# Routed experts on one core: each expert's token shares spread over its partitions by DMA from a scratch in memory, in place of three selection products per block

## The reference, cut to what matters

```
hidden[e] = silu(x @ gate[e]) * (x @ up[e])        # 64 wide
y         = sum over e of  (c[e] * hidden[e]) @ down[e]
```

## Time and profile before

| | before |
|---|---|
| median of 3 runs | 5519.05 us (5516.63 to 5520.13) |
| the profiled execution, its own time | 5518.67 us |
| its span (first to last instruction) | 5516.8 us |
| PE busy, share of the span | 4263.4 us, 77% |
| DVE busy | 3278.4 us, 59% |
| ACT busy | 2686.6 us, 49% |
| POOL busy | 1336.0 us, 24% |
| moved by DMA | 66.82 MB, 12 GB/s on average |
| mean granted TensorE clock | 0.873 |

### The profile page before, as it was taken

The page is one execution under the profiler, slowest core; times in us unless marked ns, Lnnn a source line. Parts: engine busy times, 40 slices in busy tenths (PEclk is TensorE's granted clock), DMA queues, the critical chain, the costliest instruction groups (busy, mean ns, idle before and its releaser), DMA issues. The chain is left out here.

```text
span 5516.8 us, 132549 instructions
## 1 busy us (share of the span) xinstructions
PE 4263.4 (77%) x46246; PEld 2462.1 (45%) x46246; DVE 3278.4 (59%) x5922; ACT 2686.6 (49%) x5526; POOL 1336.0 (24%) x2908
## 2 busy tenths in 40 slices
PE   2013867877669895868996578999999999999997
PEld 0002333433332221443442236666667666666665
DVE  7994434544347675434444426766666676767665
ACT  2125623545447574531111345656656565656564
POOL 0061100111101111110000044434434343434433
PEclk7556977988779897978997678999999999999998
DMA  1000000000000000000110001000000000000000
GB/s 33 0 0 3 2 19 8 1 4 1 17 19 1 1 1 12 2 14 27 30 30 12 5 1 47 6 9 23 6 14 17 5 27 5 10 23 5 27 5 11
DMA packets 46816, 66.82 MB, mean 12 GB/s; under 512 B 8628, under 2 KB 40480, under 8 KB 44977
## 3 DMA queue, kind: packets, MB, share of 16 engines
q1 hardware_dynamic: 45564, 58.16, 3.5%
q0 software_dynamic: 784, 1.80, 0.2%
HBM read 53.22 MB, written 1.05 MB: 10 GB/s over the span
## 5 line engine op out<-in xcount | busy, mean ns | idle before, releaser
L673 DVE TENSOR_REDUCE minus_max<-banks 128x1 f32<-128x512 f32 (+4 forms) x1152 | 605.7, 570 | 320.1 <-PE banks L568 312.5
L638 ACT ACTIVATE probs<-banks 128x512 f32<-128x512 f32 (+4 forms) x1152 | 581.0, 556 | 338.9 <-PE banks L606 336.5
L2766 POOL TENSOR_TENSOR loc_cos_part<-loc_cos_part,loc_sin_part 128x512 f32<-128x512 f32 x388 | 494.5, 1275 | 757.7 <-DVE loc_sin_part L3196 757.7
L2839 PE MATMUL banks<-loc_w_qkv,loc_shifted 128*128 (+1 forms) x1552 | 415.2, 414 | 94.8 <-issue 79.0
L2839 PEld LDWEIGHTS banks<-loc_w_qkv,loc_shifted 128*128 128x128 f32 x1552 | 296.0, 201 | 141.8 <-issue 97.8
L606 PE MATMUL banks<-q_stack,k_stack 64*128 64x512 bf16 (+3 forms) x1152 | 254.4, 382 | 97.6 <-DMA q_stack<-max_rows 69.6
L1320 ACT ACTIVATE gated<-banks 128x512 f32<-128x512 f32 x168 | 100.3, 597 | 448.6 <-PE banks L1276 448.6
L3193 DVE TENSOR_TENSOR loc_cos_part<-banks,loc_table 128x512 f32<-128x512 f32 x388 | 264.2, 681 | 86.4 <-ACT loc_square L3061 86.2
L3229 DVE TENSOR_TENSOR loc_headsT<-banks,loc_sum_inv 128x512 f32<-128x512 f32 x192 | 132.5, 690 | 301.1 <-ACT loc_sum_inv L3101 289.9
L3221 DVE TENSOR_REDUCE loc_minus_max<-banks 128x4 f32<-128x384 f32 x386 | 196.9, 551 | 179.2 <-PE banks L2906 178.4
L1339 DVE TENSOR_TENSOR product<-gated,banks 128x512 f32<-128x512 f32 x168 | 115.6, 688 | 308.9 <-PE banks L1278 308.9
(11 more groups left out here) (520 smaller groups left out, 9755.2 us busy)
## 6 DMA issues: line engine op xcount, KB each, us to landing
expert_w<-in_L_ffn_pairs_dram SPq DMA_DIRECT2D x84, 192.0 KB, 2.3
loc_w_qkv<-in_L_ffn_Wqkv_dram SPq DMA_DIRECT2D x7, 1536.0 KB, 8.5
q_stack<-max_rows SPq DMA_DIRECT2D x384, 3.0 KB
loc_v_edge<-loc_v SPq DMA_DIRECT2D x192, 32.0 KB, 1.8
fixed_w<-in_L_ffn_experts_dram SPq DMA_DIRECT2D x8, 514.5 KB, 4.0
loc_pack<-in_L_ffn_pack_dram SPq DMA_DIRECT2D x6, 537.5 KB, 4.9
loc_w_o<-in_L_ffn_Wo_dram SPq DMA_DIRECT2D x6, 512.0 KB, 4.3
loc_scales<-in_L_ffn_scales_dram SPq DMA_DIRECT2D x7, 256.0 KB, 8.3
```

The lines of the kernel that those rows point to most:

```text
L638: nc.scalar.activation(probs[(a % 2) * C + k][e][0:kn, q0:S], t_bank[e][0:kn, q0:S], ACT.Exp, scale=scale).then_inc(s["exp_done"], 1)
L673: nc.vector.tensor_reduce(minus_max[:, u, e, qs[0]:qs[0] + len(qs)], view, AX.X, ALU.max, negate=True).then_inc(s["max_done"], 1)
L2766: nc.gpsimd.tensor_tensor(cos_part[:, tiles, :], cos_part[:, tiles, :], sin_part[:, tiles, :], ALU.add).then_inc(s["summed"], 1)
L2839: ins = nc.tensor.matmul(g.bank[3 * j][:, (t % 2) * QK:(t % 2 + 1) * QK], xs[:, t * P:(t + 1) * P], w_qkv[:, ds(at, QK)], start=True, stop ...
```

## The change

The selection matrix, the three bf16 parts and the three products go. c is turned once, in f32, with 16 transposes, and copied out of PSUM in 4 pieces. SP writes it as rows, one for each expert and 2048 tokens long, to a scratch tensor in the chip's memory (`rows`), and waits for that. In `experts`, with the weights of a pair SP also fetches for each of its two experts the 1024 values of the current half, read 64 times over, into 64 partitions of an SBUF buffer (`expert_share`, a ring of four). DVE's second product reads that buffer in place of the third PSUM bank. DVE's loop is now rolled by four pairs, as it waits for one of four semaphores. In layer 2 three more rows repeat the shared expert's, so that 34 pairs find 68 rows.

```diff
-def spread_experts(nc, g, combine, n_experts, parts):
+def spread_experts(nc, g, combine, n_experts, n_pairs, rows):
-        split = sbuf("split", [P, 3, NT, n_experts], BF16)
-        left = sbuf("split_left", [P, NT, n_experts])
+        turned = sbuf("combine_turned", [P, T])
+        spare = 2 * n_pairs - n_experts
...
-            @block.vector
-            def _(dve):
-                chain = Chain(dve, s["split_done"])
-                chain.step(nc.vector.tensor_copy(split[:, 0], combine[:, :, :]))
-                chain.step(nc.vector.tensor_tensor(left[:, :, :], combine[:, :, :], split[:, 0], ALU.subtract))
-                chain.step(nc.vector.tensor_copy(split[:, 1], left[:, :, :]))
-                chain.step(nc.vector.tensor_tensor(split[:, 2], left[:, :, :], split[:, 1], ALU.subtract))
...
+                for b in range(B):
                     for t in range(QT):
+                        ins = nc.tensor.transpose(g.bank[b][0:n_experts, t * P:(t + 1) * P],
+                                                  combine[:, b * QT + t, :], g.ident[:, :])
                     ins.then_inc(s["turned"], 1)
...
+                for b in range(B):
+                    act.wait_ge(s["turned"], b + 1)
+                    nc.scalar.activation(turned[0:n_experts, b * S:(b + 1) * S], g.bank[b][0:n_experts, :],
                                          ACT.Copy).then_inc(s["stored"], 1)
+            @block.sync
+            def _(sp):
+                sends = 0
+                for h in range(2):
+                    cols = slice(h * (T // 2), (h + 1) * (T // 2))
+                    sp.wait_ge(s["stored"], 2 * h + 2)
+                    sp.dma_start(rows[0:n_experts, cols], turned[0:n_experts, cols]).then_inc(s["sent"], 16)
+                    sends += 1
+                    for i in range(spare):
+                        sp.dma_start(rows[n_experts + i:n_experts + i + 1, cols],
+                                     turned[n_experts - 1:n_experts, cols]).then_inc(s["sent"], 16)
+                        sends += 1
+                sp.wait_ge(s["sent"], 16 * sends)
...
-def experts(nc, g, weights, n_pairs, n_experts, parts, select, yT):
+def experts(nc, g, weights, n_pairs, rows, yT):
+        wide = [sbuf(f"expert_share{u}", [P, half]) for u in range(RING)]
-        banks = [g.bank[2:5], g.bank[5:8]]
+        banks = [g.bank[2:4], g.bank[4:6]]
...
                         sp.dma_start(w[u][:, :], weights[ds(m, 1), :, :].rearrange("a p n -> p (a n)")
                                      ).then_inc(w_loaded[u], 16)
+                        for e in range(2):
+                            sp.dma_start(wide[u][e * (P // 2):(e + 1) * (P // 2), :],
+                                         rows[ds(m * 2 + e, 1), h * half:(h + 1) * half].to_broadcast([P // 2, half])
+                                         ).then_inc(share_loaded[u], 16)
...
-                    for j in range(3):
-                        ins = nc.tensor.matmul(weight_bank[:, :], select[0:n_experts, ds(m * P, P)],
-                                               parts[0:n_experts, j, h * half + blk * S:h * half + (blk + 1) * S],
-                                               start=(j == 0), stop=(j == 2))
-                    ins.then_inc(s["weight_ready"], 1)
...
-                            dve.wait_ge(s["weight_ready"], n + 1)
-                            dve.wait_ge(s["y_done"], n + (2 * RING + 3))
-                            nc.vector.tensor_tensor(hidden[blk][:, :], product[blk][:, :], banks[blk][2][:, :],
+                            if blk == 0:
+                                dve.wait_ge(share_loaded[u], i * 32 + (total // RING + 1) * 32)
+                            dve.wait_ge(s["y_done"], i * (2 * RING) + (n + 2 * RING + 3))
+                            nc.vector.tensor_tensor(hidden[blk][:, :], product[blk][:, :],
+                                                    wide[u][:, blk * S:(blk + 1) * S],
                                                     ALU.mult).then_inc(s["hidden_done"], 1)
...
-                         (choose_f[:, :], io["c_select16"]), (buf.goes_on[:, :, :], io["c_goes_on16"])])
+                         (buf.goes_on[:, :, :], io["c_goes_on16"])])
-                    step(nc.vector.tensor_copy(select[:, :], choose_f[:, :]))
```

More of the change, by code:

```diff
@@ L1354, in grouped_experts_0 @@
         yT = sbuf("yT", [P, T])
-        parts = sbuf("combine_parts", [E, 3, T], BF16)
-        select = sbuf("expert_select", [E, E // 2 * P], BF16)
+        rows = nc.dram_tensor("grouped_rows", [E, T], F32, kind="Internal").ap()
         with ExitStack() as inner:
             sbuf = room(nc, inner)
-            w, bias, choose_f = sbuf("router_w", [P, E]), sbuf("router_bias", [P, E]), sbuf("select_f", [E, E // 2 * P])
+            w, bias = sbuf("router_w", [P, E]), sbuf("router_bias", [P, E])
             logits, scores = sbuf("router_logits", [P, NT, E]), sbuf("router_scores", [P, NT, E])
@@ L1412, in grouped_experts_0 @@
             clear(nc, s)
-            spread_experts(nc, g, scores, E, parts)
-        experts(nc, g, io["L0_ffn_pairs"], E // 2, E, parts, select, yT)
+            spread_experts(nc, g, scores, E, E // 2, rows)
+        experts(nc, g, io["L0_ffn_pairs"], E // 2, rows, yT)
         finish(nc, g, "transposed", yT)
@@ L1426, in limited_experts_2 @@
         yT = sbuf("yT", [P, T])
-        parts = sbuf("combine_parts", [C, 3, T], BF16)
-        select = sbuf("expert_select", [C, n_pairs * P], BF16)
+        rows = nc.dram_tensor("limited_rows", [2 * n_pairs, T], F32, kind="Internal").ap()
         with ExitStack() as inner:
             sbuf = room(nc, inner)
-            w, choose_f = sbuf("router_w", [P, C]), sbuf("select_f", [C, n_pairs * P])
+            w = sbuf("router_w", [P, C])
             logits, combine = sbuf("router_logits", [P, NT, C]), sbuf("combine", [P, NT, C])
@@ L1440, in limited_experts_2 @@
             running = sbuf("running", [P, NT, E], BF16)
-            load(nc, g, [(w[:, :], io["L2_ffn_router"]), (choose_f[:, :], io["c_select65"]),
+            load(nc, g, [(w[:, :], io["L2_ffn_router"]),
                          (buf.goes_on[:, :, :], io["c_goes_on64"]), (before_f[:, :], io["c_before"])],
@@ L1503, in limited_experts_2 @@
             clear(nc, s)
-            spread_experts(nc, g, combine, C, parts)
-        experts(nc, g, io["L2_ffn_pairs"], n_pairs, C, parts, select, yT)
+            spread_experts(nc, g, combine, C, n_pairs, rows)
+        experts(nc, g, io["L2_ffn_pairs"], n_pairs, rows, yT)
         finish(nc, g, "transposed", yT)
```

33 lines of the change are left out of this document (12 added, 21 removed).

## The result

The changed kernel takes 5393.55 us (median of 4 runs, 5385.81 to 5400.25), the kernel before 5518.10 us beside it (4 runs, 5516.63 to 5520.13): a ratio of 0.977, 95% interval 0.976 to 0.979. The forecast was 5389 us in a range of 5372 to 5445. The profiled execution took 5394.93 us, with a span of 5393.1 us, so 123.7 us less than before.

The account below looks back on a forecast made before the run. PE was taken to bound both expert loops. Terms 88.0 + 29.0 + 5.6 + 2.5 + 3.0 + 0.4 + 1.5 - 0.3 = 129.7 us, taken from 5518.7, gave 5389 us, range 5372 to 5445.

Parts of the forecast that it names:

- Step 1: Layer 2's loop: three selection products leave each block, period falls from 3.227 to 2.575 us, 88.0 us gained.
- The slack of 0.8 us: Layer 2's steady block: hidden ends 3.48 us after its gate product, down product due at 4.29 us.
- Rival C: A block's chain delays its down product; each block loses about 0.2 us, 33 us in all, 5422 us; chance 0.07.
- Step 2: Layer 0's loop: period falls from 3.52 to 2.575 us if gaps go with the 16-row operand; 29.0 us gained.
- rival D: Layer 0's gaps of 0.1 us stay: 9 us less gain, 5398 us; counted within the forecast's 0.68.
- Step 3: New share transfers in both loops: 2.94 us of DMA per pair within a 5.15 us period, hidden, cost zero.
- Rivals A and B: Slow share reads in the loops: A, DMA bounds but kernel gains, 5458 us, 0.12; B, kernel gets slower, 5605 us, 0.11.
- rival B: Share reads in the loops so slow that the kernel loses: 216 us lost, 5605 us; chance 0.11.
- Step 4: Before layer 2's loop: selection matrix load gone 5.6 us, its cast gone 2.5, shorter spreading 3.0 gained.
- Step 5: Before layer 0's loop: one SP issue fewer 0.4 us, shorter spreading 1.5 gained; the cast counted as nothing.
- Step 6: Three more semaphores to clear in each `experts`: -0.3 us for both layers.

Follow-up runs that it names:

- the repeat: The changed kernel run once more with no edit: 5395.46 us (median of 5), ratio 0.978 to the kernel before.

## Why the prediction was right

**Step 1** (88.0 us). Measured 87.3 us. The period, the last blocks that give nothing, and the price of 0.652 us a block all held, and the run with 65 idle rows gave the loop back. The slack of 0.8 us is 0.74 to 0.80 by the run with the added operation. Rival C had its mechanism right and its place wrong: it needs some 0.7 us more in the chain than this change has, and then costs half of the 0.2 us a block, and not in every block.

**Step 2** (29.0 us). Measured 25.4 us in the profile after and 27.8 in the repeat. That the gaps go with the 16-row operand was right (rival D is out). The term was too large by 1.2 us at best, and that lies in the first two blocks. From SP's first fetch to the first gate product after the first down product it took 10.24 us before (756.96 to 767.20) and 9.01 in the repeat, 1.2 us less where 2 x 0.945 + 0.6 = 2.5 was in the sum; the other 28 blocks gave their 0.945. Another 2.4 us is lost to PE's clock, 1.7 between the halves and 0.7 in the first blocks, which comes and goes by chance.

**Step 3** (zero). Right, and for the stated reason: the transfers fit into the period with room, and DVE never waited for a share. By the prices of a full queue a pair needs 2.96 us, where I had 2.94, but that agreement is luck: I took 2.30 us for the shares and 0.64 for the weights, where a full queue charges 2.56 and 0.40. The busy share that I had named as the sign, 57%, was 51%. With the 2.30 two sets would have needed 5.24 us, over the period of 5.15, as the double fetch then showed; the 2.03 that I read from the profile after misled my expectation. Rivals A and B needed memory to serve one row more slowly than many; the run with different rows excludes that at this load. The "factor of 3.4 below the nearest row" held against B is counted from loc_w_o; from loc_v_edge, which I had called the nearest in shape, it is 228 / 87 = 2.6. And a shape of 2 x 64 in one transfer would have brought a loss like that of rival B (5857 us, forecast 5605), by way of engines that stand idle and not of memory. The prediction had no rival for that.

**Step 4** (5.6 + 2.5 + 3.0). Measured 11.6 us in all, forecast 11.1; putting load and cast back took 8.3 of them, 6.2 for the load and 2.1 for the cast, which leaves 3.3 for the spreading. The router's first product came 4.7 us after the last issue of `load` (2423.28 to 2427.99), where I had named about 6 as a sign.

**Step 5** (0.4 + 1.5). Measured 2.6 us. The cast in layer 0 was not all covered: it cost 0.3 us where I counted nothing, and the load 0.5 where I counted 0.4. The other 1.8 us belong to the spreading, forecast 1.5.

**Step 6** (-0.3). It is below what these profiles can tell.

The steps sum to 129.7 us, the stages to 126.9 (128.4 in the repeat); step 2 alone is 3.6 too high, and steps 4 and 5 give 1.2 of it back. The difference from the medians is 5518.10 - 5393.55 = 124.6 us; the untouched stages took 3.2 and 5.2 us more in the two profiles. That is chance: the same stages took 4792 to 4806 us in the thirteen profiles of the changed kernel and its variants, in eight of them less than the 4800.3 us before.

## What to carry to other kernels

Where PE is the bound and DMA idle, a product that only spreads a row over partitions can be bought from DMA, at 2.6 us for 512 KB into two times 64 partitions on a full queue. Before writing such a transfer look at the leading dimension of its source: two rows times 64 went out in 10.6 us a pair in one transfer, and hidden in two. Price a transfer by what it takes on a full queue, not by its busy share on a half-empty one, and count a chain's slack up to a little before the product that needs its result (0.15 us here).

## What the runs showed of the hardware that I had not expected

- A transfer whose source led with 2 or 4 went as if two or four engines of sixteen carried it (shares 0.18 and 0.35, pairs of 10.6 and 5.73 us, 14 and 12 small packets fewer), and SP stood 9.4 us in its next issue.
- One row read 64 times moves as fast as 64 rows (DMA share 0.50 against 0.52, landing 4.0 us in both), on a queue with room.
- By its busy share a set of shares took 2.03 us while the queue had room (share 0.51); on a full one (1.05) each further set took 2.56 us.
- After the same 0.7 and 1.5 us of idle time PE went on at 2.4 GHz in one execution and at 1.2 GHz in another.
- Three products with a 16-row stationary operand between 128-row ones cost 0.3 us more than with 65 rows (period 3.52 against 3.23 us).
- A down product whose input was done 0.15 us or more ahead lost nothing; 0.05 to 0.09 us ahead the next product came 0.08 to 0.11 us late (67 cases in layer 2 of the run with the added operation).
